# Attention probabilities transposed by VectorE in 32x32 blocks and exchanged by SBUF transfers, with PV two heads behind the scores

## The reference

```python
xn = _layernorm(x)                                   # (1, 2048, 512)
q_nope, q_pe = q[..., :128], apply_rope(q[..., 128:]) # q = xn @ wq.T, 16 heads of 192
kv_cache = rmsnorm(kv_lat, kv_norm_w)                # (2048, 128), shared by all heads
q_lat = einsum('bshd,hdc->bshc', q_nope, wkv_b_h[:, :128])
scores = (einsum('bshc,btc->bsht', q_lat, kv_cache) + einsum('bshr,btr->bsht', q_pe, k_pe)) * 192 ** -0.5
attn = softmax(where(causal, scores, -1e30))
out_lat = einsum('bsht,btc->bshc', attn, kv_cache)   # "PV"
out = einsum('bshc,hdc->bshd', out_lat, wkv_b_h[:, 128:]).reshape(...) @ wo.T
ffn = xn @ (weight + (w_t * scale - weight)).T + bias # w_t: weight rounded to -1, 0, 1
```

## Time and profile before

| | us |
|---|---|
| median of 3 runs (lowest, highest) | 1956.49 (1955.99, 1956.75) |
| the profiled execution, its span | 1956.91, 1955.1 |
| TensorE, its weight loads busy | 1898.6, 1586.6 |
| VectorE, ScalarE, GpSimd busy | 1271.2, 889.5, 313.3 |
| mean granted TensorE clock | 0.988 |

### The profile page before, as it was taken

One profiled execution on the slowest core, in us unless ns is written; L12 is line 12 of the kernel. 1 busy time (PEld: TensorE's weight loads), 2 busy tenths in 40 slices (PEclk: granted clock), 3 DMA queues, 4 the chain that ended last, 5 costly groups with the idle time before them and its releaser, 6 DMA issues.

```text
span 1955.1 us, 32275 instructions
## 1 busy us (share of the span) xinstructions
PE 1898.6 (97%) x10350; PEld 1586.6 (81%) x10350; DVE 1271.2 (65%) x3025; ACT 889.5 (45%) x1646; POOL 313.3 (16%) x313
## 2 busy tenths in 40 slices
PE   6998999999999999999999999999999999999998
PEld 5887787778888888888888888878888888888886
DVE  4764676766666666666766666666666666666665
ACT  4554444444444444444444444444443444434443
POOL 4773212211111111011100111011010110101100
PEclk9888999999999999999999999999999999999999
DMA  6993322232111112210111101111000110001000
GB/s 207 367 333 149 119 97 81 101 140 87 54 64 54 55 69 101 87 44 35 51 43 43 43 32 54 72 57 45 22 32 32 43 32 21 32 32 43 11 11 22
DMA packets 53077, 147.46 MB, mean 75 GB/s; under 512 B 4835, under 2 KB 17380, under 8 KB 51493
## 3 DMA queue, kind: packets, MB, share of 16 engines
q1 hardware_dynamic: 52208, 145.71, 21.5%
q10 hardware_dynamic: 820, 1.15, 0.2%
HBM read 112.23 MB, written 34.60 MB: 75 GB/s over the span
## 4 chain that ended last, share of the span: by engine, by line
PE 81%; DVE 4%; issue 3%; POOL 2%; ACT 0%; DVEq 0%; POOLq 0%; ACTq 0%
PE p_score L983 31%; PE p_out L1012 18%; PE p_tr L1000 12%; PE p_lat L963 7%; PE p_tr L1023 6%; PE p_rot L963 4%; DVE rot_sin L1095 2%; PE p_out L1023 2%; DVE probs L1068 1%; PE p_score L987 1%; POOL qp_l L1234 1%; POOL qp_l L1237 1%; POOL rotated L1223 1%; DVE pT_l L1080 0%; DVE rot_cos L1091 0%
## 5 line engine op out<-in xcount | busy, mean ns | idle before, releaser
L1160 ACT ACTIVATE pT_h<-p_tr 128x512 fp32r<-128x512 f32 (+3 forms) x640 | 339.4, 532 | 790.4 <-PE p_tr L1000 788.3
L1068 DVE TENSOR_SCALAR_CACHE_REDUCE probs<-p_score 128x512 f32<-128x512 f32 (+3 forms) x640 | 388.3, 607 | 168.8 <-PE p_score L983 109.6
L1080 DVE TENSOR_TENSOR pT_l<-p_tr,pT_h 128x512 fp32r<-128x512 f32 (+3 forms) x640 | 390.2, 610 | 159.9 <-ACT pT_h L1160 153.5
L1000 PE MATMUL p_tr<-ident,probs 128*128 128x128 f32 x2176 | 343.1, 273 | 0.0
L1151 ACT ACTIVATE probs<-probs,neg_max 128x128 f32<-128x128 f32 (+15 forms) x256 | 307.5, 1201 | 70.5 <-DVE neg_max L1074 69.3
L1000 PEld LDWEIGHTS p_tr<-ident,probs 128*128 128x128 f32 x2176 | 260.5, 140 | 52.6 <-issue 0.2
L1012 PE MATMUL p_out<-pT_h,V_h 128*128 128x512 f32 (+3 forms) x640 | 274.7, 429 | 6.8 <-DVE pT_l L1080 6.8
L983 PE MATMUL p_score<-Kn_h,q_h 128*128 128x512 f32 (+3 forms) x640 | 241.4, 377 | 3.3 <-DVE q_l L1102 3.3
L983 PE MATMUL p_score<-Kp,qp_h 128*128 128x512 f32 (+3 forms) x640 | 234.5, 366 | 8.8 <-POOL qp_l L1237 8.8
L1012 PE MATMUL p_out<-pT_h,V_l 128*128 128x512 f32 (+3 forms) x640 | 234.9, 367 | 0.0
L1012 PE MATMUL p_out<-pT_l,V_h 128*128 128x512 f32 (+3 forms) x640 | 233.5, 365 | 0.0
(11 more groups left out here) (138 smaller groups left out, 2622.6 us busy)
## 6 DMA issues: line engine op xcount, KB each, us to landing
Wq<-wq_scr SPq DMA_DIRECT2D x62, 512.0 KB, 3.3
Wv<-wv_scr SPq DMA_DIRECT2D x62, 512.0 KB, 3.3
Wp<-wp_scr SPq DMA_DIRECT2D x31, 512.0 KB, 3.2
wq_scr<-Wq SPq DMA_DIRECT2D x16, 512.0 KB, 5.9
wv_scr<-Wv SPq DMA_DIRECT2D x16, 512.0 KB, 5.8
xT_scr<-xT SPq DMA_DIRECT2D x3, 2048.0 KB, 9.9
xT<-xT_scr SPq DMA_DIRECT2D x3, 2048.0 KB, 7.9
x_in<-in_x SPq DMA_DIRECT2D x4, 1024.0 KB, 7.6
```

Source lines behind the costliest of these rows:

```text
L1000: mm = pe.transpose(p_tr[k % PT_RING][:, i * P:(i + 1) * P], probs[p][:, i, k * P:(k + 1) * P], ident[:, :])
L1068: dve.tensor_scalar(probs[p][:, i, b * CW:b * CW + width], p_score[u % 2][:, 0:width], SCALE, LOWEST, ALU.mult, ALU.max, accum_out=part_ma ...
L1080: dve.tensor_tensor(pT_l[r][:, cols], p_tr[r][:, cols], pT_h[r][:, cols].bitcast(F32), ALU.subtract).then_inc(pT_split, 1)
L1160: act.activation(pT_h[r][:, cols], p_tr[r][:, cols], ACT.Copy).then_inc(pT_high, 1)
```

## The change

Notation: g counts heads over all chunks, 0 to 63.

- TensorE's transposes are gone, with their PSUM buffers `p_tr`. VectorE transposes each exp'd row block (128 queries x up to 2048 keys) in 32x32 blocks, up to eight 128-key tiles in one instruction (1024 columns), from SBUF to SBUF (`turn_row`). A 32x32 block transposed in place of its partitions leaves the 32-key quarters in the wrong partitions, so SP moves quarter to quarter: 16 transfers of 32 partitions each (`exchange`), from `turned` to `pT`. A head's exchange is one part in chunks 0 and 1, two parts (halves of the keys) in chunks 2 and 3.
- `turned` and `pT` hold 16 tiles. In chunks 0 and 1 two heads share them by halves; in chunks 2 and 3 there is one copy. So the exchange of head g waits there for PV of head g-1 up to the same tile (`free_by`), and `turn_row` of head g, row 0, for the exchange of head g-1 (`shares_turned`).
- ScalarE makes the high part of two tiles at a time from `pT` (three buffers, `high_group`), GpSimd subtracts it in place for the low part (`low_group`). VectorE's `split_tile` is gone.
- PV and the output projection of head g-2 run in step g, two tiles of PV in a unit from the first units on; there are two more steps behind the last scores. The scores have three PSUM buffers, the output projection two; `probs` is a ring of three rows.
- The latent projection, the turns, the output projections and the splits each have a unit of their own in each chunk, given by the tables below. The query is split in the last unit of chunks 0 and 1.
- Wq, Wv, cos/sin tables and `acc` have one buffer each; at a chunk change `acc` is stored before the next is loaded. GpSimd clears `turned` at the start (8192 columns).
- All loops are unrolled.

The core of the diff:

```diff
+def free_by(g, end):
+    if chunk_of(g) < 2:
+        return tiles_before(g - 1) if g >= 2 else 0
+    if g == 2 * H:
+        return tiles_before(g)
+    return tiles_before(g - 1) + min(tiles_of(g - 1), end)
+def shares_turned(g):
+    if chunk_of(g) < 2:
+        return (g - 2,) if g >= 2 else ()
+    return (g - 2, g - 1) if g == 2 * H else (g - 1,)
...
+def rotary_unit(g):
+    return (0, 1, 3, 4)[phase(g)]
...
+def latent_unit(g, it):
+    return 1 + it // 2 if phase(g) == 0 else 3 * phase(g) + it
+def query_unit(g):
+    return (3, 7, 10, 13)[phase(g)]
+def split_unit(g):
+    return (2, 4, 6, 8)[phase(g)]
+def out_unit(g, i):
+    return (3, 5 + i // 2, 8 + i, 10 + i)[phase(g)]
...
+def early_unit(g, k):
+    return units_of(g) - (1 if phase(g) == 0 else HIGH_RING - k)
+def row_unit(g, i):
+    return ((1, 2, 3), (3, 5, 7), (8, 9, 11), (11, 13, 14))[phase(g)][i]
```

Buffers, transfers and their order:

```diff
-        probs = [sb(f"probs{i}", [P, QB, S]) for i in range(2)]
-        pT_h = [sb(f"pT_h{i}", [P, CW], F32R) for i in range(PT_RING)]
-        pT_l = [sb(f"pT_l{i}", [P, CW], F32R) for i in range(PT_RING)]
+        probs = [sb(f"probs{i}", [P, S]) for i in range(ROW_RING)]
+        turned = sb("turned", [P, 4, NT, QB, 32])
+        pT = sb("pT", [P, 4, NT, QB, 32], F32R)
+        pT_h = [sb(f"pT_h{i}", [P, 4, 2, QB, 32], F32R) for i in range(HIGH_RING)]
...
-        p_score = [ps(f"p_score{i}") for i in range(2)]
...
+        p_score = [ps(f"p_score{i}") for i in range(SCORE_RING)]
+        p_result = [ps(f"p_result{i}") for i in range(2)]
...
+            def exchange(g, part):
+                first, end = part_tiles(g, part)
+                tiles = slice(tile_base(g) + first, tile_base(g) + end)
+                sp.wait_ge(blocked, QB * (g + 1))
+                need(sp, pv_done, free_by(g, end))
+                for a in range(4):
+                    for r in range(4):
+                        sp.dma_start(pT[32 * a:32 * (a + 1), r, tiles, :, :].bitcast(F32),
+                                     turned[32 * r:32 * (r + 1), a, tiles, :, :]
+                                     ).then_inc(exchanged[part][g % 2], 16)
...
+            def step(g):
+                j, h = chunk_of(g), g % H
+                if 1 <= g <= HEADS:
+                    for part in range(parts_of(g - 1)):
+                        exchange(g - 1, part)
+                if g + 2 < HEADS:
+                    load_q(g + 2)
+                if g % 2 and g + 3 < HEADS:
+                    load_rotary(g + 3)
+                if g < HEADS and j + 1 < NCH and h == H - 2:
+                    load_tables(j + 1)
+                    load_chunk(j + 1)
+                if g >= 2 and g <= HEADS:
+                    load_v(g - 1)
+                if g < HEADS and j and h == 1:
+                    store_chunk(j - 1)
+                    load_residual(j)
```

TensorE, PV and the step:

```diff
+            def values(g, k):
+                n = groups_before(g) + k // 2
...
+                    need(pe, o_split, g)
+                if k % 2 == 0:
+                    pe.wait_ge(p_low, n + 1)
+                last = k == tiles_of(g) - 1
+                i = slice(max(0, k - QB * chunk_of(g)), QB)
+                high, low = pT_h[n % HIGH_RING][:, :, k % 2, i, :], pT[:, :, tile_base(g) + k, i, :]
+                for a, (v, pt) in enumerate(((V_h, high), (V_l, high), (V_h, low))):
+                    mm = pe.matmul(p_out[:, :, i, :], v[:, k, :], pt, start=(k == 0 and a == 0),
...
+            def step(g):
+                for u in range(units_of(g)):
+                    if g < HEADS:
+                        scores(g, u)
+                    if u == rotary_unit(g) and g % 2 and g + 1 < HEADS:
+                        project_rotary(g + 1)
+                    if g >= 2 and 0 <= u - value_unit(g) < groups_of(g - 2):
+                        values(g - 2, 2 * (u - value_unit(g)))
+                        values(g - 2, 2 * (u - value_unit(g)) + 1)
+                    for it in range(IT):
+                        if u == latent_unit(g, it) and g + 1 < HEADS:
+                            project_latent(g + 1, it)
                     for i in range(QB):
-                        project_out(prev, i)
-            project_rotary((0, 0, 0))
```

VectorE's turn and step:

```diff
+            def turn_row(g, i):
+                row, tiles = QB * g + i, QB * chunk_of(g) + i + 1
+                dve.wait_ge(exped, row + 1)
+                if i == 0:
+                    for old in shares_turned(g):
+                        for part in range(parts_of(old)):
+                            dve.wait_ge(exchanged[part][old % 2], in_by(old, part))
+                if row == 0:
+                    dve.wait_ge(cleared, 1)
+                for first in range(0, tiles, 8):
+                    t8 = slice(first, min(first + 8, tiles))
+                    rows = probs[row % ROW_RING][:, P * t8.start:P * t8.stop]
+                    to = turned[:, :, tile_base(g) + t8.start:tile_base(g) + t8.stop, i, :]
+                    last = dve.transpose(to.rearrange("p a t q -> p t a q"),
+                                         rows.rearrange("p (t a q) -> p t a q", a=4, q=32))
+                last.then_inc(blocked, 1)
...
+            def step(g):
+                for u in range(units_of(g)):
+                    if g < HEADS:
+                        copy_scores(g, u)
+                    if 1 <= g <= HEADS and u == (1 if chunk_of(g - 1) else 0):
+                        turn_row(g - 1, QB - 1)
+                        invert(g - 1)
+                    if g % 2 and g + 1 < HEADS:
+                        for op in rotate_ops(g, u):
+                            rotate(g + 1, op)
+                    if g >= 2 and u == split_unit(g):
+                        split_output(g - 2)
+                    if u == query_unit(g) and g + 1 < HEADS:
+                        split_query(g + 1)
+                    for i in range(QB):
+                        if u == out_unit(g, i) and g >= 2:
+                            accumulate(g - 2, i)
+                    for i in range(QB - 1):
+                        if g < HEADS and u == row_unit(g, i):
+                            turn_row(g, i)
             for op in range(5):
-                rotate((0, 0, 0), op)
-            split_query((0, 0, 0))
```

ScalarE's and GpSimd's groups, and ScalarE's step:

```diff
+            def high_group(g, k):
+                n = groups_before(g) + k
+                tiles, i = group(g, k)
+                for part in range(parts_of(g)):
+                    if 2 * k == part_tiles(g, part)[0]:
+                        act.wait_ge(exchanged[part][g % 2], in_by(g, part))
+                need(act, pv_done, 2 * (n - HIGH_RING + 1))
+                act.activation(pT_h[n % HIGH_RING][:, :, :, i, :].rearrange("p r t i q -> p r t (i q)"),
+                               pT[:, :, tiles, i, :].bitcast(F32).rearrange("p r t i q -> p r t (i q)"),
+                               ACT.Copy).then_inc(p_high, 1)
...
+            def step(g):
+                for u in range(units_of(g)):
+                    if u == query_unit(g) and g + 1 < HEADS:
+                        high_query(g + 1)
+                    if u == rotary_high_unit(g) and g + 1 < HEADS:
+                        high_rotary(g + 1)
+                    if g >= 2 and HIGH_RING <= u - value_unit(g) + HIGH_RING < groups_of(g - 2):
+                        high_group(g - 2, u - value_unit(g) + HIGH_RING)
+                    for k in range(HIGH_RING):
+                        if 1 <= g <= HEADS and u == early_unit(g, k) and k < groups_of(g - 1):
+                            high_group(g - 1, k)
+                    if g >= 2 and u == value_unit(g) + groups_of(g - 2) - 1:
+                        high_output(g - 2)
+                    if g < HEADS and (u + 1) % (chunk_of(g) + 1) == 0:
+                        exp_row(g, u // (chunk_of(g) + 1))
...
+            def low_group(g, k):
+                n = groups_before(g) + k
+                tiles, i = group(g, k)
+                pool.wait_ge(p_high, n + 1)
+                need(pool, qp_ready, issued["rotary"])
+                low = pT[:, :, tiles, i, :].rearrange("p r t i q -> p r t (i q)")
+                high = pT_h[n % HIGH_RING][:, :, :, i, :].rearrange("p r t i q -> p r t (i q)")
+                pool.tensor_tensor(low, low.bitcast(F32), high.bitcast(F32), ALU.subtract).then_inc(p_low, 1)
+                issued["low"] += 1
```

More of the change, by code:

```diff
@@ L83, in tiles_of @@
-def tiles_of(pos):
-    return QB * (pos[0] + 1)
-def first_of_chunk(pos):
-    return isinstance(pos[1], int) and pos[1:] == (0, 0)
-def first_row(pos, k):
-    return max(0, k - QB * pos[0])
-def rotary_unit(nxt, units):
-    if nxt[2]:
-        return None
-    return units * 3 // 4 if first_of_chunk(nxt) else units // 2 - (1 if units == QB else 0)
-def walk(nc, engine, step):
-    def two_steps(j, m):
-        step((j, m, 1), (j, m, 0), (j, m + 1, 0))
-        step((j, m + 1, 0), (j, m, 1), (j, m + 1, 1))
-    for j in range(NCH):
-        step((j, 0, 0), (j - 1, H // 2 - 1, 1) if j else None, (j, 0, 1))
-        if j == 0:
```

(61 more changed lines are left out.)

422 lines of the change are left out of this document (177 added, 245 removed).

## The result

The changed kernel takes 2134.0 us (median of four runs, 2130.9 to 2143.6) where the kernel before takes 1956.6: 1.091 times as long, 95% interval 1.088 to 1.094. Slower was forecast, but at 2000 us, and 2134 lies outside the range of 1865 to 2130.

What follows compares the result with a forecast made beforehand. TensorE was taken to bound the kernel before. Chunks of 231+376+502+659 = 1768 us, adjusted to 1762, plus 184.8 before, less 2, plus 56 at the end gave 2001, stated as 2000; range 1865 to 2130.

Steps and rivals of the forecast that it cites:

- The bound now, and what goes: TensorE, 97% busy, bounds the kernel before; its 2176 transposes occupy 0.11 us each, 235 us in all.
- VectorE's turns: VectorE's 32x32-block transposes: 1.15 us at 1024 columns, 330 us for 2176 tiles.
- Rival D: VectorE's turns at half pace, adding 110 us to the forecast; chance 0.12.
- The exchange's data, 0.62 us for 128 KB: Exchange from 32 to 32 partitions: data pace of 0.62 us per 128 KB, between ends of 0.37 and 1.5.
- SP's issue spacing, 0.48 us: Exchange on SP's queue: successive issues start 0.48 us apart, so 16 transfers take at least 9.6 us.
- GpSimd "keeps up": GpSimd's low parts: 2.3 us at 1024 columns, 18 us a head in the last chunk, beside TensorE units of 2.5.
- Chunk 1: Steps of chunk 1: 23.5 us a head, 376 us in all; 21.4 a head with the exchange on time.
- Clock: TensorE's lower clock after waits, 1.2 instead of 2.4 GHz: at most 1 to 2 us a head, in the range.
- Edges: Chunk changes and end: shorter first PV -16 us, clearing and single tables some 10; the end takes 56 us.
- Rival C: Exchange data at half pace or less, 0.74 us for 128 KB: 45.1, 33.9, 25.4 us in chunks 3, 2, 1; 2137; chance 0.17.
- Rival A: Exchange issue bound, data at 0.37 us hidden behind the issues: 1907 us; chance 0.25.
- Rival B: Exchange on time everywhere, VectorE's burst alone left: 1804 us; chance 0.06.

Runs made afterwards that it cites:

- e4: The kernel before with each of the 2176 TensorE transposes made twice; 2185.6 us.
- e3: The changed kernel with seven rows of test transfers appended behind its last store; SBUF-to-SBUF issues took 0.63 to 0.64 us up to 128 KB.
- e1: The changed kernel with each exchange part as 4 transfers over 128 partitions, same bytes, key quarters not moved to their partitions; 1884.0 us.
- e5: e1 with GpSimd's low-part subtraction cut to a quarter (256 of 1024 columns); 1814.1 us.
- e6: The changed kernel with ScalarE's exp of a head's last row moved behind the fourth group's high part in chunks 1 to 3; 2095.8 us.
- e10: The changed kernel with half the exchange on ScalarE's queue (chunks 2, 3), last exp later (chunk 3), chunk 1's latent projection and query split earlier; 1905.8 us.
- e11: The changed kernel with as many exchange transfers, each moving only the first half of its tiles; 2112.7 us.

## Why the prediction missed, point by point

- **The bound now, and what goes**: held. 0.106 us a transpose (e4), 230 us in all against 235.
- **VectorE's turns**: held. 341.8 us busy against 330 (1024 columns 1.235 us each, where the forecast has 1.15; 128 columns 0.29, so 1.05 ns a column, as for its other operations). Rival D falls. **ScalarE** held: 1.05 for a group of 1024 columns, under the 1.14; but it is now the least loaded of all, since GpSimd has 1003.5 us busy and ScalarE 851.5.
- **The exchange's data, 0.62 us for 128 KB**: held, and it was the guess I trusted least; 0.63 to 0.65 in e3. The Trainium skill, SBUF — State Buffer, section Door 1: The DMA port swizzle, gives 189 GB/s for half of the ports at 1 MiB; e3's fifth row, 256 KB each within 32 partitions, has 189 GB/s as well, the last landing of some 2 us included.
- **SP's issue spacing, 0.48 us**: this is the step that failed. It came from three plain loads and was treated as a fact of the queue, with no upper bound, while the data beside it had a range of 0.37 to 1.5. The trace of the kernel before had dearer issues: its 128 KB loads of wkb (L280) are 0.42 to 1.23 us long, 0.64 in the median. The exchange's issues start 0.63 us apart alone, and 0.65 (chunk 2) and 0.68 (chunk 3) in the mean of a run of 32. In chunk 2 the forecast lets 17.3 us pass from first issue to last landing (24.6-7.3); it was 22.2: 4.9 us of the 6.1 by which the step is longer, 79 of 97 us over 16 heads. The other 1.2 lie between the last landing and the next first issue, 15.3 us against 14.1 (5.4+1.4+7.3). In chunk 3, 23.3 us against 21.8, made up in part by 18.8 against 19.4 behind it. In chunk 0 the issues are not what was missing: with a quarter of them (e1) it keeps its 15.1 us a head.
- **GpSimd "keeps up"**: right in pace (2.38 us in the mean at 1024 columns, 2.3 when they follow each other), wrong as a cost of nothing. Its shorter subtraction is worth 70 us on the way from 1884 to 1814 (e1, e5), 39 of them in chunk 3 and 16 in chunk 0, where it accounts for the 0.7 us a head over the forecast and more (13.7 in e5). The fourth group's hand-over in a step costs a wait of 2.3 us and clock, 38 us in the changed kernel (e6). In the forecast this was hidden by the exchange standing above it in chunks 2 and 3, but it delays the exchange's start in chunk 3.
- **Chunk 1**: 23.3 against 23.5, but with its mechanism only in part, so the agreement is partly luck: with the exchange as good as free it has 22.3 (e1) where the forecast has 21.4 on time, and the earlier query gives back 0.95 of 1.8 (e10).
- **Clock**: "1 to 2 us a head at most", left out of the sum. It was 43 us over chunk 2 (2.7 a head) by e1's comparison. Much of it lies inside a wait, but not all: in the step shown, ten 512-column matmuls take from 1117.8 to 1122.1, most starts 0.43 us apart instead of 0.23, which is 2.0 us more ahead of the PV that releases the exchange. That is enough for the 1.2 us above; no run shows it by itself.
- **Edges**: the chunks are 11 us longer than 16 steady steps each (-9 to +14 by chunk), where -6 was forecast. The end took 56 us, as forecast.

The sum: 11 (chunk 0) -4 (chunk 1) +97 (chunk 2) +17 (chunk 3) +17 (edges) = 138 us, of the 140.6 between the spans of 2001 and 2141.6. The price of an issue is 79 of it in chunk 2; what the 17 us of edges are made of, no run shows.

**Rival C** named 2137 us and would look confirmed by the total. It is not: it put the data at 0.74 us and had 25.4, 33.9 and 45.1 us a head in chunks 1 to 3, where 23.3, 37.5 and 42.3 were measured; e3 and e11 rule it out. Rival A (issue bound at the price of the loads, 1907) had the right resource at the wrong price. Rival B's 1804 came out at 1884 with GpSimd whole and 1814 without its hand-over.

Of what was to be seen: VectorE's wait for the exchange before row 0 is there, but longer in chunk 2 than the 4 to 5 us forecast (6.1 to 9.8 in heads 4 to 15; 3.3 to 7.0 in chunk 3). TensorE busy near 1600 is not (1793.0): the same matmuls are longer at the lower clock, but e5, with a granted clock of 0.98, still has 1674.5, so 1600 was too low by itself; "issues 0.48 apart, the last landing 20 us after the first" is what the trace refuted at first sight.

What stays open: why an issue from SBUF costs more than one from HBM, and what chunk 0 loses at its edges (254.5 us for the chunk in the changed kernel, 234.7 in e5 with 13.7 us a head, 231.6 before with 14.4). No run takes the two-buffered output projection back.

## What to carry to other kernels

Price a transfer's issue from a transfer of the same kind, and give it a range as wide as the data's: up to 128 KB the SBUF-to-SBUF transfers here took as long to issue as to move or longer, and a second queue for half of them gave back 166 us here. Before costing a helper engine at nothing because it is half idle, follow its first piece in each step: what stands ahead of it on its producer, and what waits behind its consumer. A total that agrees with a rival proves nothing until the stages agree too.

## What the runs showed of the hardware that was not expected

- An SBUF-to-SBUF transfer takes 0.63 us to issue at 16 and at 128 KB alike, and over 32 or 128 partitions (0.94 at 256 KB, 1.05 at 512 KB); HBM to 32 partitions 0.46 alone and 0.51 in a run of 32 in the kernel; the 512 KB weight loads 0.33, but 0.58 right behind a run of the exchange.
- 4.19 MB within SBUF took 12.0 us over 128 partitions, 22.2 us from 32 to 32, and 20.3 us when consecutive transfers alternate between the halves: alternating gives next to nothing back.
- With TensorE idle for 7.4 us a head (118 us over chunk 2) the granted clock of the whole chunk was 0.88 and its matmuls were busy for 473 us; with 5 us of idle time in all (e1) it was 1.00, and the same matmuls 430 us.
